# Moving the values product to the end of a step, one sine operation per q or k, and a first preparation placed in the last steps of the stack before it

## The reference, cut to what matters

```python
# x: 4 sequences of 1024 tokens, 128 channels
x = x + 0.5 * ffn_ref(layernorm(x))
x = x + attn_ref(layernorm(x))
x = x + 0.5 * ffn_ref(layernorm(x))      # the same weights again

def ffn_ref(x):                          # two layers; 8 heads of 64, window 64
    for l in range(2):
        h = shift_token(x)
        q, k, v = split(h @ wqkv[l])     # 128 -> 3 * 512
        q, k = l2norm(q) * qs, l2norm(k) * ks
        q = q*cos*scale + rotate_half(q)*sin*scale   # k: divided by scale
        x = x + local_attention(q, k, v) @ wo[l]     # own and previous window
        h = layernorm(shift_token(x)) * g + b
        a, g = split(h @ w1[l] + b1)     # 128 -> 2 * 341
        x = x + (a * gelu(g)) @ w2[l] + b2
    return x

def attn_ref(y):                         # full attention over 1024 tokens
    k, q, v = (layernorm(y @ W + b) * gain + beta for each)
    return softmax(k @ q.T) @ v + y
```

## Time and profile before

| what | value |
|---|---|
| median of 3 runs | 1849.92 us |
| profiled execution, its own time | 1851.99 us |
| its span, first to last instruction | 1850.2 us |
| mean granted PE clock | 0.952 |
| busy: PE / DVE / ACT / POOL | 1532.3 / 1326.1 / 1176.9 / 1099.0 us |

### The profile page before, as it was taken

How to read it: one execution, slowest core, us unless ns; L and a number is a source line. 1 busy time by engine, 2 the same in 40 slices (tenths; PEclk the granted TensorE clock), 3 DMA queues, 4 the chain that set the end, 5 groups by cost and what they waited for, 6 DMA issues and landing times.

```text
span 1850.2 us, 44040 instructions
## 1 busy us (share of the span) xinstructions
PE 1532.3 (83%) x15864; PEld 1241.0 (67%) x15864; DVE 1326.1 (72%) x3419; ACT 1176.9 (64%) x2460; POOL 1099.0 (59%) x1130
## 2 busy tenths in 40 slices
PE   1789999978899999655788978899998899999984
PEld 1577777767777777532566657777776677777763
DVE  6687979776879787523445358887877778878773
ACT  1576767665767676514655747776766667767671
POOL 3685858574868585403323257766756667768560
PEclk9999999999999999865989899999999999999997
DMA  8241222222222121040000042121223121212113
GB/s 277 47 124 43 52 50 58 57 81 62 59 50 52 46 52 42 20 140 23 24 23 12 23 110 51 43 56 39 64 50 94 45 73 42 56 42 60 46 28 115
DMA packets 183670, 112.46 MB, mean 61 GB/s; under 512 B 86720, under 2 KB 164128, under 8 KB 182944
## 3 DMA queue, kind: packets, MB, share of 16 engines
q1 hardware_dynamic: 183456, 109.65, 22.7%
HBM read 43.41 MB, written 23.42 MB: 36 GB/s over the span
## 4 chain that ended last, share of the span: by engine, by line
PE 51%; DVE 24%; ACT 11%; issue 6%; SPq 3%; DMA 3%; POOL 2%; DVEq 0%; ACTq 0%; POOLq 0%
PE QK L372 9%; PE TO L613 8%; PE TO L680 5%; PE QK L613 5%; DVE rope_c L1018 5%; DVE rope_s L1023 4%; DVE o_n L1043 4%; DVE top L962 3%; PE TO L372 3%; PE SC L654 3%; DVE h2n L1030 3%; ACT probs L1180 3%; PE TO L780 2%; PE VB L780 2%; PE TO L726 2%
## 5 line engine op out<-in xcount | busy, mean ns | idle before, releaser
L1180 ACT ACTIVATE probs<-SC,shift,qgain 128x128 f32<-128x128 f32 x1024 | 390.7, 481 | 103.4 <-DVE shift L970 103.3
L1347 POOL TENSOR_TENSOR ve<-mv,epsilon 128x1 f32<-128x1 f32 x128 | 24.5, 192 | 404.1 <-DVE mv L1009 404.1
L372 PE MATMUL QK<-w_qkv,hT 128*128 128x512 f32 x768 | 220.3, 423 | 20.0 <-DMA w_qkv<-qkv_d 10.9
L1018 DVE TENSOR_TENSOR rope_c<-QK,rope 128x512 f32<-128x512 f32 x256 | 175.5, 686 | 77.1 <-PE QK L372 74.4
L1360 POOL TENSOR_TENSOR rnorm<-clip,mhalf 128x8 f32<-128x8 f32 x128 | 211.1, 1649 | 12.1 <-DVE clip L979 12.0
L1369 POOL TENSOR_TENSOR qgain<-clip,mhalf 128x8 f32<-128x8 f32 x128 | 209.5, 1637 | 0.0
L613 PE MATMUL TO<-ident,probs 128*128 128x128 f32 x1280 | 191.5, 277 | 18.7 <-ACT probs L1180 10.1
L962 DVE TENSOR_REDUCE top<-SC 128x4 f32<-128x512 f32 x256 | 174.6, 682 | 28.8 <-PE SC L654 28.6
L1174 ACT ACTIVATE v_own<-VB 128x512 f32<-128x512 f32 x128 | 76.5, 598 | 182.7 <-PE VB L372 182.7
L1023 DVE TENSOR_TENSOR rope_s<-QK,rope 128x256 f32<-128x256 f32 x512 | 190.5, 413 | 0.0
L613 PEld LDWEIGHTS TO<-ident,probs 128*128 128x128 f32 x1280 | 154.9, 143 | 52.3 <-issue 32.9
(11 more groups left out here) (147 smaller groups left out, 3775.6 us busy)
## 6 DMA issues: line engine op xcount, KB each, us to landing
v_prev<-v_own SPq DMA_DIRECT2D x256, 130.0 KB, 2.3
x_att<-stream SPq DMA_DIRECT2D x128, 64.0 KB, 2.2
h<-stream SPq DMA_DIRECT2D x256, 32.0 KB, 1.9
stream<-x_new SPq DMA_DIRECT2D x32, 256.0 KB
w_qkv<-qkv_d SPq DMA_DIRECT2D x3, 1536.0 KB, 7.4
h<-x_mid SPq DMA_DIRECT2D x128, 32.0 KB
h<-x_mid SPq DMA_DIRECT2D x128, 31.8 KB
rope<-rope_d SPq DMA_DIRECT2D x24, 128.0 KB, 3.2
```

The lines of the kernel that those rows point to most:

```text
L372: last = mm(dst, fr(left(a)), fr(right(b)), start=(k == 0), stop=(k == 2))
L1018: v.tensor_tensor(qk(rope_c[:])[:, m], src, rope[:, i, m, 0:1, :].to_broadcast([P, HEADS, DH]), ALU.mult)
L1180: last = nc.scalar.activation(probs[:, b, hd, :], SC[:, hd * P:hd * P + P], ACT.Exp, bias=shift[:, b, hd:hd + 1], scale=qgain[:, b, hd % 4 ...
```

## The change

Inside a step:

- On PE the values product moves from behind the k product to the end of the step, ahead of the turn of `o_n`. The turns of `h` and `h2n` go into TT (columns 0 to 255) in place of VB. TT is also where the probabilities are turned, so the first half of the probabilities now waits for `s_hl` and `s_h2l` of the step before, and the first pair of a burst waits for both too.
- On ACT the copy of `v_own` moves from behind the exponentials of half 1 to behind the copies of hT and h2T, ahead of oT, kT, qT.
- On DVE the low parts of hT and h2T move ahead of the squared norms. The sine part is one operation of 512 elements per q or k, which reads the two halves of each head through a view with a negative step.

Between stack 0 and the attention: the preparation of sequence 0 is placed in hooks (`after`) behind the last seven steps of stack 0, in other buffers (`x_2b`, `pT2`, `z_0` in v_own, banks SC and QK), and `AHEAD` empty rows become one. `stack_done` is waited for by ACT alone, ahead of its first write of `x_new`. In the attention, for the other sequences, DVE's input stage moves ahead of the row's maximum, and ACT's normalising groups change places with the row's copy or exponentials. The ones in `v_own` are set again in row 4, since z_0 overwrites them.

```diff
# the loop around a step: a hook after every step; the last steps of a stack are counted from DRAIN
-        if g == 1 and after_two:
-            after_two()
+        if after:
+            after(g)
 
 
 AHEAD = TILES + 1
+DRAIN = NT + QKV
...
-    return s if r == 0 and 0 <= s < SEQS else None
+    return s if r == 0 and 1 <= s < SEQS else None
...
# sync
+                def half_step_loads():
+                    sp.dma_start(x_2b[:], rows(x_in[0])).then_inc(g_ld, 16)
+                    sp.dma_start(v_g[:], rows(stream[DEPTH, 0, 1:, :])).then_inc(g_ld, 16)
+
+                iteration(ITERS - 1, () if k else [(0, half_step_loads)])
...
+                if k == 0:
+                    sp.dma_start(x_att[:], rows(x_in[1])).then_inc(g_ld, 16)
+                    sp.wait_ge(s_o, NT)
+                    sp.dma_start(x_h1, rows(stream[DEPTH, 1, 1:, :])).then_inc(g_ld, 16)
...
# TensorE, inside a step
                     if t := tile(ATT):
+                        if t2 := tile(TH + 1):
+                            pe.wait_ge(s_hl, t2.count())
+                        if t2 := tile(FFN_IN + 1):
+                            pe.wait_ge(s_h2l, t2.count())
                         probs_transposed(t, 0)
...
-                        if t2 := tile(FFN_IN + 1):
-                            pe.wait_ge(s_h2l, t2.count())
-                        if before is not None:
-                            pe.wait_ge(s_xn, before * 2 + 1)
-                        product(mm, VB[:], lambda x: hT[:, b, x, :], lambda x: w_qkv[:, x, 1024:1536]).then_inc(s_v, 1)
...
-                        need(pe, s_vown, t.count(back=1))
                         need(pe, s_hl, t.count(back=1))
-                        transpose(VB[:, 0:P], h[:, t.i % 4, :]).then_inc(s_th, 1)
+                        transpose(TT[:, 0:P], h[:, t.i % 4, :]).then_inc(s_th, 1)
                     if t := tile(FFN_IN):
                         pe.wait_ge(s_h2n, t.count())
-                        if t2 := tile(QKV):
-                            pe.wait_ge(s_vown, t2.count())
-                        else:
-                            pe.wait_ge(s_h2l, t.count(back=1))
-                        transpose(VB[:, P:2 * P], h2n[:, t.i % 2, :]).then_inc(s_th2, 1)
+                        need(pe, s_h2l, t.count(back=1))
+                        transpose(TT[:, P:2 * P], h2n[:, t.i % 2, :]).then_inc(s_th2, 1)
+                    if t := tile(QKV):
+                        b = t.i % 2
+                        need(pe, s_vown, t.count(back=1))
+                        if before is not None:
+                            pe.wait_ge(s_xn, before * 2 + 1)
+                        product(mm, VB[:], lambda x: hT[:, b, x, :], lambda x: w_qkv[:, x, 1024:1536]).then_inc(s_v, 1)
...
# TensorE, the feed-forward burst
+                    if k == 0:
+                        pe.wait_ge(s_h2l, last_in.count())
+                        if t := tile(TH):
+                            pe.wait_ge(s_hl, t.count())
+                    if k == 1 and n == ITERS - 1:
+                        pe.wait_ge(g_z, TILES)
                     if k == 1 and (t := tile(QKV)):
                         pe.wait_ge(s_rot, t.count())
                         pe.wait_ge(s_sq, t.count())
-                    if k == 3:
-                        pe.wait_ge(s_h2l, last_in.count())
...
-                        if t := tile(TH):
-                            pe.wait_ge(s_hl, t.count())
+                        if t := tile(QKV):
+                            pe.wait_ge(s_vown, t.count())
...
# TensorE, hooks in the last steps of the first stack
+            def after(g):
+                if g == DRAIN + 2:
+                    pe.wait_ge(g_yn, 1)
+                    pe.wait_ge(s_p, NT * 2)
+                    for half in range(2):
+                        for i in range(HALF):
+                            last = transpose(SC[:, half * 512 + i * P:half * 512 + i * P + P], pT2[:, half * HALF + i, :])
+                        last.then_inc(g_ty, 1)
+                if g == DRAIN + 3:
+                    for i in range(TILES):
+                        if i < 4:
+                            pe.wait_ge(g_yT, 2)
+                        else:
+                            pe.wait_ge(g_z, i - 3)
+                        dst = QK if i % 4 >= 2 else SC
+                        mm(dst[:, i % 2 * 512:i % 2 * 512 + 384], y_T[:, i * P:i * P + P],
+                           w_kqv[:, :, :].rearrange("p a b -> p (a b)"), start=True, stop=True).then_inc(g_pr, 1)
+                if g == DRAIN + 5:
+                    for m, dst in ((0, SC), (1, QK)):
+                        pe.wait_ge(g_zn, m + 1)
+                        for half in range(2):
+                            for i in range(HALF):
+                                last = transpose(dst[:, half * 512 + i * P:half * 512 + i * P + P],
+                                                 z_0[:, half * HALF + i, m * DIM:m * DIM + DIM])
+                            last.then_inc(g_tk, 1)
+
+            pipeline(step(0), 0, after)
+            pe.wait_ge(s_xn, ITERS * 2)
+
+            for g in range(-1, ROWS + 2):
...
# VectorE, hooks and rotation
+            def after(g):
+                if g == DRAIN - 1:
+                    joined(0)
+                if g == DRAIN:
+                    joined_stats(0, range(HALF))
+                if g == DRAIN + 1:
+                    joined_moments(0, joined_stats(0, range(HALF, TILES)))
+                if g == DRAIN + 3:
+                    for i in range(4):
+                        shifted_in(0, i)
+                if g == DRAIN + 4:
+                    z_stats(0, TILES - 1)
+                    z_moments(0)
...
-                        sin = rope[:, i, m, 1:2, :]
-                        for half in range(2):
-                            a, o = 32 * half, 32 * (1 - half)
-                            last = v.tensor_tensor(qk(rope_s[:])[:, m, :, a:a + 32], src[:, :, o:o + 32],
-                                                   sin[:, :, a:a + 32].to_broadcast([P, HEADS, 32]), ALU.mult)
+                        sin = rope[:, i, m, 1:2, :].rearrange("p o (a d) -> p o a d", a=2)
+                        last = v.tensor_tensor(qk(rope_s[:])[:, m].rearrange("p h (a d) -> p h a d", a=2),
+                                               src.rearrange("p h (a d) -> p h a d", a=2)[:, :, ::-1, :],
+                                               sin.to_broadcast([P, HEADS, 2, 32]), ALU.mult)
...
-                if t := tile(QKV):
-                    b = t.i % 2
-                    dve.wait_ge(s_sq, t.count())
-                    need(dve, s_rn, t.count(back=2))
-                    v.tensor_reduce(norm2[:, b, :], sq[:].rearrange("p (h d) -> p h d", d=DH), AX, ALU.add).then_inc(s_n2, 1)
                 if t := tile(TH):
                     b = t.i % 2
                     dve.wait_ge(s_hT, t.count())
                     if t2 := tile(FFN_IN):
                         dve.wait_ge(s_h2T, t2.count())
                     need(dve, s_v, t.count(back=2))
-                    v.tensor_tensor(fr(hT[:, b, 1, :]), VB[:, 0:P], hT[:, b, 0, :], ALU.subtract).then_inc(s_hl, 1)
+                    v.tensor_tensor(fr(hT[:, b, 1, :]), TT[:, 0:P], hT[:, b, 0, :], ALU.subtract).then_inc(s_hl, 1)
                 if t := tile(FFN_IN):
                     dve.wait_ge(s_h2T, t.count())
                     own = slice(t.i * P, t.i * P + P)
-                    v.tensor_tensor(fr(h2T[:, 1, own]), VB[:, P:2 * P], h2T[:, 0, own], ALU.subtract).then_inc(s_h2l, 1)
+                    v.tensor_tensor(fr(h2T[:, 1, own]), TT[:, P:2 * P], h2T[:, 0, own], ALU.subtract).then_inc(s_h2l, 1)
+                if t := tile(QKV):
+                    b = t.i % 2
+                    dve.wait_ge(s_sq, t.count())
+                    need(dve, s_rn, t.count(back=2))
+                    v.tensor_reduce(norm2[:, b, :], sq[:].rearrange("p (h d) -> p h d", d=DH), AX, ALU.add).then_inc(s_n2, 1)
+                if burst == ITERS - 1:
+                    for i in range(4, TILES):
+                        shifted_in(0, i)
+                    z_stats(0, 0)
                 if burst is not None:
                     n = burst
                     for k in range(6):
+                        if n == ITERS - 1:
+                            z_stats(0, k + 1)
...
+                if (s := prepared(g, 0)) is not None:
+                    input_stage(s)
...
# ScalarE: the copy of v_own now stands behind those of hT and h2T; hooks
+            def after(g):
+                if g == DRAIN + 2:
+                    y_normalised(0)
+                    y_moved(0, 0)
+                    y_moved(0, 1)
+                if g == DRAIN + 4:
+                    z_normalised(0, 0)
+                    z_normalised(0, 1)
+                if g == DRAIN + 5:
+                    for m in range(2):
+                        z_moved(0, m, 0)
+                        z_moved(0, m, 1)
```

(63 more changed lines are left out.)

152 lines of the change are left out of this document (71 added, 81 removed).

## The result

| | before | after |
|---|---|---|
| median of 4 runs | 1849.80 us (1848.46 to 1853.71) | 2205.77 us (2205.42 to 2213.46) |
| ratio, 95% interval | | 1.193 [1.190, 1.196] |
| profiled span | 1850.2 us | 2203.8 us |
| mean granted PE clock | 0.952 | 0.908 |
| busy: PE / DVE / ACT / POOL | 83 / 72 / 64 / 59% | 76 / 63 / 54 / 50% |

The forecast was 1820 us. The work between the stacks did get shorter, by 42.5 us; each stack got longer by some 197 us. No engine's share has grown, so every step waits for something. (In microseconds PE was busy for 132 us more and DVE for 55 more. PE ran at a lower granted clock: over the first 4 us of the burst's products it was 0.50 to 0.61 in 12 of the 14 bursts between sequences, before 1.00 in all.

The account below looks back on a forecast made before the run. Two nearly equal loops, PE's (9.12 us) and POOL with DVE's (9.20), were taken to bound the ordinary step. Handover -40, steps +14, attention -4 gave -30 from 1852.0: 1822, as a median 1820 us; range 1780 to 1845.

Parts of the forecast that it names:

- the sentence on the copy of `v_own`: ACT inside a step: the copy moved ahead of oT moves oT from 314.18 to 314.68, output product 0.20 us late.
- a loop through the new waits: Among the other cases (0.05 together): steps of 9.5 us and more, taking away the handover's gain, near 1850 us.
- Handover -40 and attention -4: Between stacks: first score row at 818.3, -40 us (-31 to -47); attention sequences 1 to 3: -4 us (-9 to +9).
- some 22 us behind the last gated product: Sign that the forecast is right: the attention's first score row starts some 22 us behind stack 0's last gated product.
- Ordinary step 9.33: Step without burst: output product 0.10 to 0.20 us late, 0.14 taken on the POOL and DVE loop, giving 9.33 us.
- Rival 1: DVE's second shift slips in ahead of POOL's q_r: mean step 8.9 us, 1778 us in all; chance 0.16.
- Sine 0: DVE's sine as one operation saves 0.10 us per step, but DVE waits longer for the same q_r: taken at 0.
- Burst +0.4: A burst's first pair on PE waits for both low parts: 0.4 us taken, bounds 0 and 1.05.
- The steps together: Both stacks: +18 us over 14 full sequences, -4 for first steps of each stack (the fill), together +14.
- Rival 3: DVE's sine reads the reversed view at half speed: every step about 1.2 us longer, 1954 us; chance 0.04.
- Rival 4: POOL's qgain holds DVE's first shift as well: some 1.2 us more per step, 1954 us; chance 0.01.
- Rival 2: The drain between stacks grows by 20 to 25 us, not 9: handover gain 25, 1835 to 1840 us; chance 0.12.

Follow-up runs that it names:

- the kernel with two sine operations: Changed kernel with the h2 DMAs ahead of v_prev on SP's queue, sine part taken back to two operations of 256: 1867.2 us, ratio 1.011 to the kernel before.
- the shift-first kernel: Changed kernel with h2 first on SP's queue and, on DVE, half 1's maximum and shift directly behind half 0's: 1843.4 us, ratio 0.9975 to the kernel before.

## Why the prediction was wrong

**The step that failed**, the path that the copy of `v_own` opens on SP, is in the sentence on the copy of `v_own`: "oT moves from 314.18 to 314.68", "kT, qT move too". It priced what stands behind the moved copy on ACT and never asked who waits for the copy. SP does, in every step, with three DMAs behind that wait that don't need it; the prediction mentions SP only for its added loads. The numbers were to be had: the new place of the copy is behind that of h2T, about where oT stood (314.2); copy 0.6, five issues 3.3, landing 2.2 give 320.3, where `bn_stats` starts some 0.3 us ahead of `x_mid` (316.25), 4.3 us too late, every step. The forecast gave "a loop through the new waits" 0.05 together with other cases and looked for it among PE's waits only; its range ended 361 us short.

With that one order mended, the changed kernel took 1843.1 us, inside the range and 23 over the forecast. Term by term:

- *Handover -40 and attention -4: right in the sum, by parts less so.* From the last rotation of stack 0 to the first of stack 1 the kernel with `h2` in front takes 291.8 us, before 336.1: -44.3. All of it is the handover: from the last gated product to the first score row are 13.0 us in place of 62.1 (forecast 13.5), and the drain ahead of it is 5.1 us longer (forecast 9), together -44.0. The attention's -4 is -0.3. The sign "some 22 us behind the last gated product" counted the drain twice; the forecast's own sum gives 13.5. In the kernel with the handover alone the median fell by 41.
- *Ordinary step 9.33: right once SP's order is mended*, 9.35 (12.55 as the kernel stood), and by the mechanism named: second shift held by `q_r` (1.25 us), `h2n` free (0.34), PE idle ahead of the probabilities. The tie was as near as the forecast said: the shift is issued 0.03 us behind `q_r`'s start. Rival 1 (the shift slips ahead) needs an edit and then brings 9.13, not 8.9.
- *Sine 0: mis-sized*, 11 to 24 us. The pair itself saves 0.065 us, near the 0.05 taken; the error is in "taken at 0". The forecast had both halves of the reason, that `h2n` is held when issued 0.08 us ahead of `k_r` and free at 0.15, and that the edit brings `h2n` forward by 0.10. It followed the gain only to the second shift. Its 9.33 counted `h2n` as free in the changed step, so in the sum the error stayed hidden; taken apart, the sine is what frees it.
- *Burst +0.4: mis-sized* by the clock. With `h2` in front the first pair of a burst waits 1.67 us for the low part of h2T in 12 of 14 bursts (0.98 and 1.41 in two), above the forecast's bound of 1.05. In four of the 12 the granted clock of the next 4 us is 0.57 to 0.62, in the others 1.00 (windows of two bursts of that kernel: stretch, length, busy times, granted clock, DMA share, GB/s):

```profile
252.00:256.00 4.00, 3.99 (x11) 3.17 (x12) 1.79 (x2) 1.80 (x3) 0.73 (x1) 0.57 0.28 67
...
343.30:347.30 4.00, 3.99 (x17) 3.08 (x18) 2.54 (x3) 2.49 (x4) 0.73 (x1) 1.00 0.28 67
```

  That is 1.2 GHz for most of the first stretch and 2.4 for the second; PE had been idle 1.67 us ahead of both. It makes a burst step 25.5 us in place of 24.0, four times: +6. At the full clock the burst step is 24.0 us (before 23.7 to 24.0) and the one behind it 9.68 (before 9.47), so there +0.4 was about right.
- *Layer change: missing from the sum.* `v_own` comes later in the step, and `w_qkv` and `w_o` stand behind it on SP. PE's waits for these two are 15.7 and 8.0 us with `h2` in front, 10.9 and 5.8 before. The four sequences around the two changes take 395 us in place of 383: +12, of which some 5 are their share of the longer ordinary steps. The other 7 are what PE's two waits grew by (23.7 in place of 16.7).
- *The steps together* were to be +14 (+18 with -4 for the fill); the two stacks, first to last rotation, grew by 13.1 and 17.0: +30. The layer change (+7) and the clock in the bursts (+6) are most of the difference; what is left, +17, stands against the forecast's +14. -44 + 30 = -14, the profiled span of that kernel less the one before, 16 over the forecast of -30. The medians are only 7 us apart, which makes the 23: the profiled execution was the fastest of ten, 5 us below their median, and that of the kernel before 2 us above its own.
- *Rival 3 (reversed view at half speed): wrong*, 680 ns against 686 for the cosine. *Rival 4 (`qgain` holds the shift): wrong.* In the kernel with two sine operations the first shift starts at 327.37, inside `qgain` (326.61 to 328.25), and takes 0.16. *Rival 2 (drain longer by 20 to 25): wrong*, 5.1.

## What to carry to other kernels

When a copy is moved, list everyone who waits for it, and on each in-order queue the items behind that wait, DMA issues first: here three DMAs that didn't need the copy cost 363 us, and reordering five issues gave them back. Put on a DMA queue first what is ready first; even where ordinary steps hide it, the loads of the next phase stand behind (15 to 18 us here). A saving of 0.13 us per step that the forecast took at 0 decided whether one engine's operation got in ahead of another's, ended 0.8 us of standing still, and took 0.14 to 0.15 us off the step. So follow a small gain to the first such race and not only to the end of the loop.

## What the runs showed of the hardware

- Each of the five DMA issues of a step takes 0.49 to 0.84 us of SP's queue, so that they are 3.3 us in a row, more than the copy of `v_own` and the landing together (0.66 + 2.16).
- A DVE operation of 128x4 is held for the whole of a POOL operation of 128x512 (`q_r`: 1.25 us in place of 0.16), and `h2n` likewise by `k_r` (1.11 in place of 0.34); POOL's operation of 128x8 (`qgain`, 1.64 us long) did not hold a `shift` that started inside it (0.16). Being 0.20 us ahead of `k_r` was enough for `h2n` (and 0.15 in the earlier trace rows), 0.03 us behind `q_r` the `shift` was held.
- After the same idle time of PE, 1.67 us, the clock was granted in full over the next 4 us in eight bursts and at 0.57 to 0.62 in four, the second and the sixth burst of each stack. In the kernel with two sine operations it was idle for only 0.99 us ahead of most bursts, and the clock was 0.57 after it in eight of 12; in the shift-first kernel, with 0.21 us at most, it was 1.00 in every burst. So the length of this idle time alone does not tell the cases apart; what does I did not find.
